# A perceiver layer with quantised FFN: weights quantised in the first tile, softmax division on ScalarE, keys of the next batch ahead of the transposes of P

## The reference, cut to what matters

```python
# x (64, 32, 512); ctx (64, 257, 512); mask (64, 1, 1, 257); H = 16 heads of 32
# 1. cross attention, then residual
xn = layernorm(x)
q, k, v = xn @ Wq + bq, ctx @ Wk + bk, ctx @ Wv + bv          # split into 16 heads
p = softmax(q k^T / sqrt(32) + mask * -1e9)
x1 = x + (p v) @ Wo + bo
# 2. Mamba block, then residual
xz = layernorm(x1) @ in_proj_w;  x_, z = split(xz)             # 1024 channels each
x_ = silu(causal conv of 4 taps over the 32 positions + conv_b)
B, C, d = split(x_ @ x_proj_w)                                 # 16, 16, 1 columns
dt = softplus(d * dt_w + dt_b);  dA = exp(dt * -exp(A_log))
h_t = dA_t * h_(t-1) + dt_t * x_t * B_t;  y_t = h_t . C_t      # 32 steps, 16 states
x2 = x1 + ((y + x_ * D) * silu(z)) @ out_proj_w
# 3. FFN on uint8 activations (one scale per tensor) and int8 weights (one scale per row)
s_w = max|w[f, :]| / 127;  wq = clip(round(w / s_w), -128, 127)
out = x2 + qlinear(relu(qlinear(layernorm(x2), w1, b1)), w2, b2)   # 512 -> 2048 -> 512
```

## Time and profile before

| | us |
|---|---|
| median of 3 runs | 2852.68 (2851.47 to 2855.08) |
| the profiled execution | 2854.31 |
| its span, first to last instruction | 2852.5 |

### The profile page before, as it was taken

How to read it: one execution, slowest core, us unless ns; L and a number is a source line. 1 busy time by engine, 2 the same in 40 slices (tenths; PEclk the granted TensorE clock), 3 DMA queues, 4 the chain that set the end, 5 groups by cost and what they waited for, 6 DMA issues and landing times.

```text
span 2852.5 us, 34374 instructions
## 1 busy us (share of the span) xinstructions
PE 2263.9 (79%) x10476; PEld 1604.0 (56%) x10476; DVE 2357.5 (83%) x3229; ACT 1416.2 (50%) x3798; POOL 293.8 (10%) x313
## 2 busy tenths in 40 slices
PE   6988888888888888788888888888888888631287
PEld 4665656565665666565656656665656566320133
DVE  2259898998979797988989797979889798989776
ACT  1245454635464554536354645545363546363283
POOL 1001001001000000100010000001000000015003
PEclk9999999999999899999899998999998999765598
DMA  6010100101010101001010101011010101120013
GB/s 195 28 52 21 48 30 20 53 14 64 11 60 19 59 20 48 31 32 39 13 64 11 60 19 59 20 48 30 26 46 13 64 11 57 54 102 0 22 67 103
DMA packets 70557, 123.55 MB, mean 43 GB/s; under 512 B 15968, under 2 KB 35056, under 8 KB 67376
## 3 DMA queue, kind: packets, MB, share of 16 engines
q1 hardware_dynamic: 70448, 122.44, 13.0%
HBM read 109.43 MB, written 12.99 MB: 43 GB/s over the span
## 4 chain that ended last, share of the span: by engine, by line
DVE 52%; PE 20%; issue 15%; ACT 7%; DMA 4%; DVEq 1%; POOL 0%; SPq 0%; ACTq 0%; POOLq 0%
DVE hb L1315 15%; DVE hb L1324 11%; DVE hb L1318 7%; PE bank L783 6%; DVE hb L1311 6%; PE bank L713 4%; ACT dA L995 3%; DMA BC<-bcd_dram 2%; PE bank L847 2%; DVE xs L1273 2%; DVE Pr L1225 2%; DVE oT L1238 2%; PE bank L812 1%; DMA bcd_dram<-bcd 1%; PE bank L688 1%
## 5 line engine op out<-in xcount | busy, mean ns | idle before, releaser
L995 ACT ACTIVATE dA<-dt,A_sb 128x124 f32<-128x124 f32 x2048 | 604.5, 386 | 70.3 <-DVE hb L1315 70.3
L1315 DVE TENSOR_TENSOR_SCAN hb<-dA,hb 128x2048 f32<-128x2048 f32 x128 | 566.1, 4423 | 32.6 <-ACT dA L995 30.4
L697 PE MATMUL bank<-wv_sb,ctxT 128*128 128x512 f32 x1024 | 501.2, 638 | 3.1 <-ACT ctxT L889 3.1
L688 PE MATMUL bank<-ctxT,wk_sb 128*128 128x256 f32 x2048 | 457.5, 381 | 0.0
L688 PEld LDWEIGHTS bank<-ctxT,wk_sb 128*128 128x128 f32 x2048 | 385.2, 190 | 63.1 <-issue 7.7
L783 PE MATMUL bank<-xn2T,win_sb 128*128 128x128 f32 x2048 | 309.3, 325 | 72.0 <-ACT hb L940 61.1
L783 PEld LDWEIGHTS bank<-xn2T,win_sb 128*128 128x128 f32 x2048 | 301.9, 239 | 84.5 <-ACT hb L940 66.9
L697 PEld LDWEIGHTS bank<-wv_sb,ctxT 128*128 128x128 f32 x1024 | 210.8, 212 | 232.1 <-issue 216.2
L713 PE MATMUL bank<-KT,Qd 128*128 128x257 f32 x512 | 174.7, 474 | 207.7 <-DVE soft L1213 204.6
L1324 DVE TENSOR_TENSOR hb<-hb 128x1024 f32<-128x1024 f32 (+2 forms) x384 | 325.7, 848 | 11.6
L1318 DVE TENSOR_TENSOR hb<-hb,BC 128x2048 f32<-128x2048 f32 x128 | 293.1, 2290 | 3.4
(11 more groups left out here) (141 smaller groups left out, 2659.9 us busy)
## 6 DMA issues: line engine op xcount, KB each, us to landing
ctx_sb<-in_ctx_dram SPq DMA_DIRECT2D x64, 512.0 KB, 3.8
BC<-bcd_dram SPq DMA_DIRECT2D x16, 2048.0 KB, 9.7
maskb<-in_mask_Bx1x1xS_fk_dram SPq DMA_DIRECT2D x64, 128.5 KB, 3.2
h_sb<-in_L_ffn_w_dram SPq DMA_DIRECT2D x2, 4096.0 KB, 16.2
x_sb<-in_x_dram SPq DMA_DIRECT2D x16, 256.0 KB, 2.7
win_sb<-in_L_attn_in_proj_w_dram SPq DMA_DIRECT2D x1, 4096.0 KB, 20.0
x_dram<-x SPq DMA_DIRECT2D x16, 256.0 KB, 2.9
xn_dram<-xn3T SPq DMA_DIRECT2D x16, 256.0 KB, 2.7
```

The costliest lines, as they stand in the source:

```text
L688: last = pe.matmul(bank[2 + j][:, (m % 2) * KF:(m % 2 + 1) * KF], wk_sb[:, c, m * P:(m + 1) * P], ctxT[:, c, :], start=(c == 0), stop=(c = ...
L697: last = pe.matmul(bank[h][:], ctxT[:, c, h * P:(h + 1) * P], wv_sb[:, c, :], start=(c == 0), stop=(c == DC - 1))
L995: last = act.activation(dA[:, c % 2, n * BT:(n + 1) * BT, 1:], dt[:, c, :].rearrange("p (b s) -> p b s", s=S)[:, :, 1:], ACT.Exp, scale=A_ ...
L1315: ins = dve.tensor_tensor_scan(flat, dA[:, c % 2].rearrange("p n s -> p (n s)"), flat, 0.0, ALU.mult, ALU.add)
```

## The change

1. The weights are quantised in interval 0. They come in four pieces of 4096 words per partition to two staging tiles that lie over Mamba's (not yet used) tiles. On DVE: the row maximum of absolute values (place c), scale (place p), round in two halves (places d and e, or a of the next stage). SP stores the bf16 pieces to DRAM; at the start of the last interval they are loaded back, and only the transposes stay there. ACT's Abs and POOL's part are gone.
2. The division of the softmax goes from DVE to ACT (`normalise`). Scores are made negative (Wq times -1/sqrt(32), mask +1e9), DVE takes the minimum, so ACT can use it as bias at once with scale -1, one group m at a time; DVE's negation (L1218) is gone. The bias of V goes into the bias of Wo; the copy into `oT` goes from DVE to ACT.
3. `kv_keys(g + 1)` stands ahead of `transpose_p(g)`; in b = 0 `kv_transpose` stands ahead of `mamba_bcd`. The transposes of P write banks 4 and 5 (the last column, now one transpose, bank 3), the value product bank 2, bcd bank 6.
4. V has one buffer: ACT's copies of V of g + 1 wait for P times V of g. `DECAYS` are moved, and the last key's four one-row products become one product with 4 rows.

```diff
-        DECAYS = {(0, "o"): (0,), (0, "q"): (1,), (1, "b"): (2,), (1, "c"): (3,), (2, "b"): (4,),
-                  (2, "c"): (5,), (3, "b"): (6,), (3, "d"): (7,)}
+        DECAYS = {(0, "o"): (0,), (0, "q"): (1,), (1, "c"): (2,), (1, "q"): (3,), (2, "c"): (4,),
+                  (2, "q"): (5,), (3, "c"): (6,), (3, "d"): (7,)}
...
+                    if ta is not None:
+                        part.normalise(g)
                     if start:
                         if tail:
                             part.out_sum(tm - 1)
-                        part.mamba_bcd(tm, ta)
-                        part.mamba_silu(tm, 0)
                         if following:
                             part.kv_transpose(g + 1, ta - 1)
                             if not isinstance(g, int) or g + 2 < B:
                                 part.load_context(g + 2)
+                        part.mamba_bcd(tm)
+                        part.mamba_silu(tm, 0)
+                    if following:
+                        part.kv_keys(g + 1, ta if b == 0 else 0)
                     place("b")
-                    if following and not start:
-                        part.kv_values(g + 1, (b + 1) % 2, 0)
                     if ta is not None:
-                        part.transpose_p(g, ta if b == 0 else 0)
+                        part.transpose_p(g, following)
                     if start:
                         part.mamba_gate(tm, 1)
                         part.mamba_silu(tm, 1)
-                    elif following:
-                        part.kv_values(g + 1, (b + 1) % 2, 1)
+                    if following and not start:
+                        part.kv_values(g + 1, 0)
                     place("c")
...
                     if start and following:
-                        part.kv_values(g + 1, (b + 1) % 2, 0)
-                        part.kv_values(g + 1, (b + 1) % 2, 1)
+                        part.kv_values(g + 1, 0)
                     place("p")
                     if following:
-                        part.kv_keys(g + 1, ta if b == 0 else 0)
+                        part.kv_values(g + 1, 1)
                     place("q")
...
-                def transpose_p(self, g, t):
-                    pe.wait_ge(p_ready, DC * (g + 1))
-
-                    wait(pe, bcd_copied, t)
+                def transpose_p(self, g, following):
+                    pe.wait_ge(scored, DC * (g + 1))
                     for h in range(2):
                         for m in range(DC):
-                            last = pe.transpose(bank[2 + h][:, m * P:(m + 1) * P], Pr[:, m, h * P:(h + 1) * P], idf[:])
+                            pe.wait_ge(p_ready, DC * g + m + 1)
+                            last = pe.transpose(bank[4 + h][:, m * P:(m + 1) * P], Pr[:, m, h * P:(h + 1) * P], idf[:])
                         last.then_inc(pt_psum, 1)
-                    for m in range(DC):
-                        last = pe.transpose(bank[4][0:1, m * P:(m + 1) * P], Pr[:, m, KF:KEYS], idf[:])
-                    last.then_inc(pt_psum, 1)
+
+                    pe.wait_ge(k_copied, DC * (g + 2) if following else DC * (g + 1))
+                    pe.transpose(bank[3][0:DC, 0:P], Pr[:, :, KF], idf[:]).then_inc(pt_psum, 1)
...
-                def kv_values(self, g, r, h):
-
-                    wait(act, o_psum, g - 1)
+                def kv_values(self, g, h):
+
+                    wait(act, o_psum, g)
                     act.wait_ge(v_psum, 2 * g + h + 1)
-                    act.copy(V[:, r, h, :], bank[h][:]).then_inc(v_copied, 1)
+                    act.copy(V[:, h, :], bank[h][:]).then_inc(v_copied, 1)
...
                 def softmax(self, g):
-                    act.wait_ge(neg_ready, g + 1)
                     for m in range(DC):
-                        act.activation(Pr[:, m, :], Pr[:, m, :], ACT.Exp, bias=soft[:, 1, m:m + 1],
-                                       accum_out=soft[:, 2, m:m + 1]).then_inc(exp_done, 1)
-
-                def transpose_p(self, g, t):
+                        act.wait_ge(scored, DC * g + m + 1)
+                        act.activation(Pr[:, m, :], Pr[:, m, :], ACT.Exp, scale=-1.0, bias=soft[:, 0, m:m + 1],
+                                       accum_out=soft[:, 1, m:m + 1]).then_inc(exp_done, 1)
+
+                def normalise(self, g):
+                    act.wait_ge(recip_done, g + 1)
+                    for m in range(DC):
+                        act.mul(Pr[:, m, :], Pr[:, m, :], soft[:, 2, m:m + 1]).then_inc(p_ready, 1)
```

More of the change, by code:

```diff
@@ L94, in perceiver_kernel @@
         xn3T = sb("xn3T", [P, DC, P])
+        before_mamba = taken[0]
         xs = sb("xs", [P, IC, P])
@@ L99, in perceiver_kernel @@
         bcd = sb("bcd", [2 * NS + 1, P])
+        before_rows = taken[0]
         BC = sb("BC", [P, 2 * NS + 1, P])
@@ L327, in place @@
                             part.scans(tm, SCANS[b].get(name, ()))
[L329 to L333, removed]
+                            if last and (b, name) == (1, "c"):
+                                part.weights_transpose(0)
                             if last and (b, name) == (2, "c"):
[L335 to L338, removed]
                                 part.weights_transpose(1)
+                        else:
+                            part.weights_prepare(b, name)
                     if start:
@@ L708, in scores @@
                         if m == 1:
-                            wait(pe, o_copied, HC * g)
+                            if isinstance(t, int) and t == 1 and b == 0:
+                                pe.wait_ge(bo_ready, 1)
                         if m >= 2:
@@ L736, in weigh_values @@
                         for h in range(2):
-                            pe.matmul(o, V[:, r, h, m * P:(m + 1) * P], PT[:, h, m, :], start=(h == 0), stop=False)
-                        last = pe.matmul(o, vlast[0:1, m * P:(m + 1) * P], PTl[0:1, m, :], start=False, stop=True)
+                            last = pe.matmul(bank[2][:, m * P:(m + 1) * P], V[:, h, m * P:(m + 1) * P],
+                                             PT[:, h, m, :], start=False, stop=(m == DC - 1 and h == 1))
                     last.then_inc(o_psum, 1)
@@ L741, in wo_product @@
                 def wo_product(self, t, more):
-                    if isinstance(t, int) and t == 0:
+                    first = isinstance(t, int) and t == 0
+                    if first:
                         pe.wait_ge(w_loaded, 16 * OTHER_DMAS)
                     pe.wait_ge(o_copied, HC * BT * (t + 1))
-                    if more:
-                        pe.wait_ge(k_copied, DC * BT * (t + 1) + DC // 2)
                     for m in range(DC):
-                        last = pe.matmul(bank[2][:], oT[:, m, :], wo_sb[:, m, :], start=(m == 0), stop=(m == DC - 1))
@@ L750, in wo_product @@
-                    last.then_inc(wo_psum, 1)
+                        last = pe.matmul(bank[2][:], oT[:, m, :], wo_sb[:, m, :], start=(m == 0),
+                                         stop=(m == DC - 1 and not first))
+                    if first:
+                        for m in range(DC):
+                            last = pe.matmul(bank[2][:], bqkv[:, 2, m:m + 1].broadcast_to([P, P]), wo_sb[:, m, :],
+                                             start=False, stop=(m == DC - 1))
+                    last.then_inc(wo_psum, 1)
@@ L752, in q_product @@
+                    if first:
+                        for m in range(DC):
+                            last = pe.matmul(bank[5][:], bqkv[:, 2, m:m + 1].broadcast_to([P, P]), wo_sb[:, m, :],
+                                             start=(m == 0), stop=(m == DC - 1))
+                        last.then_inc(bvo_psum, 1)
                 def q_product(self, t):
@@ L1080, in mamba_pad @@
                     pool.wait_ge(last_psum, 1)
+                    if isinstance(t, int) and t == 0:
+                        pool.wait_ge(wq_stored[3], 16)
                     apart(pool)
```

267 lines of the change are left out of this document (151 added, 116 removed).

## The result

The changed kernel takes 3103.96 us (median of 4 runs, 3102.25 to 3104.85) against 2853.11 of the kernel before on the same chip (2851.47 to 2855.08): ratio 1.0878, 95% interval 1.0859 to 1.0897. It is slower by 251 us, and 3071 had been forecast.

A forecast was written before the change was run, and what follows sets the result against it. DVE was taken to set the pace in b = 1 to 3, a chain through all engines in b = 0. From 2854.3 us, +267 for the tiles, -53 for the last interval and +3 for interval 0 gave 3071 us, range 3000 to 3150.

The forecast's parts named there:

- The last interval, -53: Last interval: its 32 steps fall from 150.2 to 96.8 us as the weight work leaves, saving 53 us.
- Interval 0, +3: First interval, bound by PE: wider Wo products +7.2, smaller value products -4.4, DVE's weight work hidden; about 3 us lost.
- b = 1 to 3, the hold through ACT's order: Full tiles: decays behind V copy 0, which waits for P times V, delay DVE's scans; +3.5, +3.6, +1.2 us.
- The term for the clock, +0.9: Keys in b = 1 to 3: PE's lower clock after its wait adds 0.9 us, from a range of 0 to 7.
- b = 0, +9.9: Stage b = 0 of a full tile: the keys hold the front of Mamba, first decays 9.9 us later (0 to 17).
- all three steps: b = 0: bcd +4.8 behind context transposes; Abs +8.6 through gate 1 behind keys; first decays +9.9 with ACT's oT copies.
- That DVE stays the pace (2682): Rival: DVE paces b = 1 to 3, b = 0 isn't lengthened, so freed work comes out; 2682 us, chance 0.12.
- that only b = 0 is real (2950): Rival: only the hold in b = 0 costs time, b = 1 to 3 break even; 2950 us, chance 0.13.
- That the lower clock covers all keys (3351): Rival: PE's longer waits put all keys in b = 0 to 2 at the lower clock; 3351 us, chance 0.05.
- More table loads or a drain behind each (3110): Rival: ACT in b = 0 loads more tables or drains after loads, 2.6 us a tile, +39; 3110 us, chance 0.04.
- The division on ACT at nothing: ACT's four division products run while PE is at the keys, so cost nothing; without the keys there, 0.4 us.
- What would show it: Signs: scan waits some 20 us a tile, PE idle 3 before bcd, gate 1 11 later, DVE busy -160, tiles 175.

The follow-up runs named there:

- E8: The kernel before with the early weight quantisation alone: 2790.17 us, ratio 0.9783 to the kernel before.
- E1: The changed kernel with the decays of chunks 2, 4 and 6 ahead of the Exps, not behind the first V copy: 2952.93 us.
- E6: The changed kernel with two buffers of V, decays left in their place: 2999.92 us.
- E3: The changed kernel with bcd and the first gate Silu ahead of the context transposes again in b = 0: 3016.84 us.
- E7: The changed kernel with the division and the copies into oT back on DVE: 3108.18 us.
- E5: The changed kernel with three orders undone (decays early; bcd first and keys behind V in b = 0): 2770.43 us, ratio 0.9722 to the kernel before.

## Why the prediction was right, and where not

- **The last interval, -53: right.** The 32 steps take 96.80 us, in the same view as rows 9, the number that was worked out; DVE's sum is at 2.41 again, as POOL has nothing to do there.

```profile
2836.80:2933.60 96.80, 12.88 (x112) 8.76 (x112) 93.02 (x57) 54.81 (x167) 0.00 (x0) 0.55 0.01 3
```

- **Interval 0, +3: right in sum (+4.2), wrong in its parts.** DVE's 37 us of new work were taken as hidden, and its stall for x's second tile (12.65 us) wasn't seen: the step that prices what moves must count the bytes too. Against it, each later batch saved 2.2 us (20.85 for 23.09), where 1.1 was forecast, and the keys, now first, ran while DVE waited for x, which the prediction didn't count. That the sum came out at +4.2 is luck; E8, with the weights but without the new order, is at +15.2.
- **b = 1 to 3, the hold through ACT's order: right.** +3.7, +3.6 and +0.4 against +3.5, +3.6 and +1.2. E1 and E6 show the mechanism, that the decays stand behind a V copy which stands behind P times V. The scan of step 9 starts 24.3 us after the stage (24.1 forecast). The term for the clock, +0.9, was too low, as the keys took 8.80 for 7.1; transposes and P times V, some 0.6 us shorter than counted, hid most of that, so the size agrees in part by luck. E1 got some of it back, in b = 2 (8.86 to 7.63). In b = 3 the scan of step 25 starts 24.2 us after the stage, as forecast (24.1), with no wait ahead of it: DVE's own work, held up 3.32 us by the transposes of P, and the decays both end at 1726.9.
- **b = 0, +9.9: right in all three steps, low in size; it was +12.6.** The bcd start came 5.4 us later (forecast 4.8), gate 1 13.9 (11.1), Abs 11.5 (8.6). The term that was too small is the clock. It is worth 2.5 us: bcd took 3.62 for 1.94 us (granted clock 0.50) and the keys 7.96 for 7.1 (0.90). The prediction had no clock term for bcd, and for the keys it took 0 out of a range of 0 to 7, because gate 1 behind PE's long work is at full clock. But bcd and the keys stand behind PE's new waits of 2.37 and 3.04 us, and gate 1 (3.81) doesn't. E3 takes the waits away, and bcd and the keys are back at 1.94 and 7.17. Times 13 tiles this is 33 us; less the 0.6 a tile by which b = 1 to 3 stayed below their forecast, it is most of the 29 us by which tiles 2 to 14 exceed theirs.
- **Tile 1 and tile 15: right** (+16.4 and +15.5 for +15 and +15).
- **The rivals.** That DVE stays the pace (2682) and that only b = 0 is real (2950) fall to the 4.55 us before steps 9 and 17. That the lower clock covers all keys (3351) falls by degree: the keys took 8.80 and 7.96 at a mean granted clock of 0.80 and 0.90, between the two levels (0.50 and 1.00 in these rows). More table loads or a drain behind each (3110) lies nearest the measured time, and is wrong all the same. ACT loads tables 65 times in either kernel, so the K copies between two Silus cost no load; and ACT's Silu L1004 ends at 1614.73, and the load, at 1614.75, takes 1.28 and is followed at 1616.04.

```profile
1614.75 1.28 ACT L1008 ACT_TABLE_LOAD   x1
1616.04 0.20 ACT L1008 ACTIVATE consts<-consts 128x1 f32<-128x1 f32 x1
```

  The Trainium skill (ScalarE: Activation LUTs, What ACT_TABLE_LOAD costs) adds a drain of about 1.4 us to each load; these rows leave 0.02 us ahead of the load and 0.01 behind it, and show none.
- **The division on ACT at nothing: right.** The four products take 1.71 us on ACT against 1.34 on DVE, the keys cover them, and E7 finds no gain in undoing it.
- **What would show it**, as it had been put: full tiles 177.5 (175 forecast), PE idle 3.04 us before bcd (3), gate 1 later by 13.9 (11), DVE's busy time less by 164 (160), but scan waits of 184 us in total or 12 a tile and not 20, as the rest of the late time shows as waits for Ln (5.48) and for the transposes of P (7.95 in b = 0, 1.6 in b = 1).

## What to carry to other kernels

In a program whose engines each run one list in order, ask of every moved call what it now stands ahead of on each engine: three such places turned a change that is worth -80 us (E5) into +251. Work taken off the busiest engine is only worth something if no wait takes its place; read the first long wait of that engine and follow it two engines back. A wait that is put ahead of TensorE's work can cost twice, once as the wait and once as the slower work behind it (bcd here: 3.04 us of waiting, then 3.62 for 1.94).

## What the runs showed of the hardware

**VectorE's two-input instructions hold GpSimd.** POOL's scaling of the mask took 0.52 us on average before and takes 2.49 in the changed kernel (from the costliest groups):

```profile
L1091 POOL TENSOR_SCALAR maskn<-maskb 128x257 f32<-128x257 f32 x64 | 159.5, 2493 | 5.4
```

It is the same instruction. POOL and DVE in b = 1 of the changed kernel:

```profile
1641.34 2.21 POOL L1088 COPY KT<-klastT 128x4 f32 x1 [26.70 <-DVE soft L1270]
1643.63 4.53 POOL L1091 TENSOR_SCALAR maskn<-maskb 128x257 f32<-128x257 f32 x1
1641.21 2.29 DVE L1353 TENSOR_TENSOR hb<-u,BC 128x2048 f32<-128x2048 f32 x1
1643.53 4.42 DVE L1357 TENSOR_TENSOR_SCAN hb<-dA,hb 128x2048 f32<-128x2048 f32 x1
```

A copy of 4 columns takes 2.21 us and ends (1643.55) as DVE's product does (1643.50); the mask's scaling ends (1648.16) as the scan does (1647.95). Both DVE instructions read two tensors in SBUF. In E7 DVE's division stands between them, with one tensor input, and POOL is through at once:

```profile
1642.44 0.41 POOL L1075 TENSOR_SCALAR maskn<-maskb 128x257 f32<-128x257 f32 x1
1642.43 1.35 DVE L1262 TENSOR_SCALAR Pr<-Pr,soft 128x257 f32<-128x257 f32 x4
```

The Trainium skill (GPSIMD Engine Reference, Specifications) says that GpSimd shares its SBUF interfaces with VectorE and contends with instructions in a 2-port mode or with two SBUF inputs. The rows agree, and give the size: in both, POOL came second and was through within 0.3 us of the end of DVE's instruction. The other way round it is rows 10: the first of DVE's three instructions takes 26.13 of the 27.32 us beside POOL's 29.72, and ends (2602.82) 1.5 us before POOL's does (2604.33). Here the mask is needed a stage later, so POOL's 127 us more cost nothing.

**TensorE's keys are slower behind waits, but not by the length of the last one.** The same 32 matmuls of the keys, with the mean granted clock over them:

| | wait of PE ahead | keys | clock |
|---|---|---|---|
| E3, b = 0 | 0.75, right ahead of the keys | 7.17 | 1.00 |
| E1, b = 2 | 5.84, ahead of the scores before them | 7.63 | 0.93 |
| changed kernel, b = 0 | 2.37 ahead of the context transposes and 3.04 ahead of bcd | 7.96 | 0.90 |
| changed kernel, b = 1 | 8.07, ahead of the scores | 8.80 | 0.80 |
| changed kernel, b = 2 | 7.22, ahead of the scores | 8.86 | 0.79 |
| E1, b = 3 | 2.73, ahead of the scores | 8.86 | 0.80 |

In E5 the same wait of 2.7 us in b = 3 has keys of 7.17 us behind it in one tile (clock 1.00) and of 8.86 in another (0.81). What decides between them these traces don't show. The mean granted clock of the whole span, 0.842 in the changed kernel and 0.860 in E1, goes with the time; but E5, which is faster than the kernel before, is at 0.886 and the kernel before at 0.890.
